# Two gated FFN blocks in one kernel: transposes of x and h moved from TensorE to VectorE blocks and DMAs

## The chip, the cores and the metric

One core of a Trainium2 chip runs the whole program. The metric is the device time of one execution in microseconds; the figure of a kernel is the median of its runs. TensorE is called PE, VectorE DVE, ScalarE ACT, GpSimd POOL, and SP (SyncE) issues the DMAs.

## The reference

x has 4 x 512 tokens of 512 values, 2048 rows in all. Two blocks follow each other, each of the form x + layernorm(FFN(layernorm(x))):

```python
def first(x):                                  # w_gate, w_up: 1376 x 512, w_down: 512 x 1376
    s = silu(x @ w_gate.T)
    s = set_to_zero(s, the 688 of each row's 1376 values with the smallest |s|)
    return (s * (x @ w_up.T)) @ w_down.T
def second(x):
    return (silu(x @ W_gate.T) * (x @ W_up.T)) @ W_down.T
x = x + layernorm(first(layernorm(x)))
x = x + layernorm(second(layernorm(x)))
```

All of it is float32. The selection by rank in the first block is exact.

## The kernel before, in words

**Precision.** A float32 matrix product is made of three fast ones: each operand is split into a high part (rounded by ACT) and a low part (the rest, subtracted by DVE), and hi x lo, lo x hi and hi x hi are added up in PSUM. So each operand costs an ACT instruction and a DVE instruction before PE can read it.

**First block.** The 2048 rows are 16 tiles of 128 tokens (`TILES`). For tile j: x is loaded into `xin` (two buffers), normalised (`x_stats`, L860; `x_normalise`, L871; POOL's `x_rstd`, L1193, in between), turned by four PE transposes into PSUM (`transpose_x`, L391), split into `xT` (`split_x_hi`, L632; `split_x_lo`, L877). `product(j, m, n)` (L404, matmuls at L418) makes gate (m=0) and up (m=1) in three column pieces n, 12 matmuls each, into a ring of four PSUM banks `gu_ps`. `silu` (L625) writes the gate into `prod` (two buffers), `abs_values` (L919) writes |s|, then a search for the 688th value runs: six passes `count` (L608) on ACT with two POOL instructions (`newton`, L1217) after each of five of them, then `find_below`, `find_top`, `find_flag` (L970, L976, L980) on DVE. `times_up` (L925) multiplies by up, and `select` (L1006, instruction at L1013) zeroes what is below the threshold, so that `prod` holds h. h is turned by eleven PE transposes into three PSUM banks `tr_ps` (`transpose_h`, L422, instruction at L432), split into the single buffer `hT` (`split_h_hi`, L647; `split_h_lo`, L888), and multiplied by w_down in 33 matmuls (`down`, L436, matmuls at L447) into the bank `y_ps`. Then come layernorm (`y_stats`, L895; `y_rstd`, L1200; `normalise_y`, L655), residual (`add_residual`, L904) and a store to a scratch tensor in HBM.

**Second block.** 16 tiles again, in four groups of four. Here the weights are the stationary operand, so h comes out turned already (`chunk`, L452, matmuls at L468; `down2`, L472, matmuls at L489). Only x has to be turned: four PE transposes per tile, into a bank of the ring. The weights of this block are loaded over those of the first (`load_pairs`, L272, from a copy that `copy_raw`, L264, made during the first block) and split on the way.

**Order of the work.** Nothing is scheduled by a program: each engine has its list of calls written out by hand, and semaphores tie them together. In the steady part of the first block (L524) PE's list for tile j is gate 0, gate 1, `transpose_h(j-2)`, gate 2, `down(j-2)`, `transpose_x(j+1)`, up 0, up 1, up 2. DVE's list is at L1084, ACT's at L740, POOL's at L1246 and SP's at L328. Tiles 11 to 14 (`TWO`) also prepare one x tile of the second block's first group each; the order in which x tiles are prepared is `XSEQ`.

Of the kernel before, what the change touches and what calls it, by code (L numbers as in the profile page):

```python
# [16 lines left out]
def sandwich(nc, x, w_gate, w_up, w_down, W_gate, W_up, W_down, out):  # L17
    B, S, H = x.shape
    I = w_down.shape[0]
# [29 lines left out]

    xf = x.rearrange("b s h -> (b s) h")  # L50
# [32 lines left out]

    def width(j):
        return P if j < JC - 1 else LASTJ

    ctx = ExitStack()
    with ctx:
# [26 lines left out]
        prod = sb("prod", [P, 2, IP])  # L115
# [46 lines left out]
        def h_place(idx):  # L162

            place = idx % 4
            if place < 2:
                return xT[:, place, 0, :], xT[:, place, 1, :]
            at = 2 * (place - 2) * GW
            flat = hT[:, :, :].rearrange("p s i -> p (s i)")
            return flat[:, at:at + GW], flat[:, at + GW:at + 2 * GW]
# [21 lines left out]
        g_done, u_done, x_tr, h_tr, y_done = map(sem, ("g_done", "u_done", "x_tr", "h_tr", "y_done"))  # L191
# [13 lines left out]
        half_done = sem("half_done")  # L205
        exact = sem("exact")
# [7 lines left out]

        ring = [("G", 0, 0), ("G", 0, 1), ("G", 0, 2), ("G", 1, 0), ("G", 1, 1), ("G", 1, 2)]
# [3 lines left out]
        X_AT = {2: 0, 4: 1, 6: 2, 8: 3}  # L219
        for g in range(GROUPS):  # L220
            for j in range(JC):
                ring += [("g", g * JC + j, 0), ("u", g * JC + j, 0)]
                if j in X_AT and g < GROUPS - 1:
                    ring.append(("X", TILES + GT * (g + 1) + X_AT[j], 0))
        place = {what: k for k, what in enumerate(ring)}

        def bank(what):
            return gu_ps[place[what] % 4]

        def x_bank(a):  # L230

            if ("X", a, 0) in place:
                return bank(("X", a, 0))
            return tr_ps[1] if a == 1 else tr_ps[2]

        @block.sync
        def _(sp):
# [3 lines left out]
            def load_x(a):  # L241

                p = POS[a]
                if p >= 2:
                    sp.wait_ge(x_tr, p - 1)
                if a >= TILES:
                    sp.wait_ge(stored[a % 2], 16 * ((a - TILES) // 2 + 1))
                src = rows(xf, a) if a < TILES else rows(x1, a - TILES)
                sp.dma_start(xin[:, p % 2, :], src).then_inc(x_in[p % 2], 16)

            def load_w(w):
# [7 lines left out]
                else:  # L259
                    size = P if n + c < JC else LASTJ  # L260
                    src = w_down[n * P:n * P + (c - 1) * P + size, :].rearrange("(c q) h -> q c h", q=size)
                    sp.dma_start(stage[0:size, slot, 0:c, :], src).then_inc(stage_in[slot], 16)
# [9 lines left out]
            def load_pairs(m):  # L272
# [4 lines left out]
                for k, (j, n) in enumerate(PAIRS):  # L277
# [46 lines left out]
            for w in range(12, NP):  # L324
                load_w(w)
            load_res(0)
            load_res(1)
            for j in range(2, TILES - 1):  # L328
                load_x(XSEQ[POS[j + 1] + 1])
                if j >= 4:  # L330
                    load_res(j - 2)
                if j in TWO:
                    load_x(XSEQ[POS[j + 1] + 2])
                store(j - 2)
                if j >= 3:
                    copy_raw(j - 3)
# [3 lines left out]
            load_pairs(1)  # L340
            store(TILES - 3)
            load_res(TILES - 2)
            store(TILES - 2)
# [3 lines left out]
            load_x(TILES + 6)  # L347
            load_x(TILES + 7)
            for g in range(GROUPS):
                b = TILES + GT * g  # L350
                if g > 0:
# [6 lines left out]
                    if g < GROUPS - 1:  # L358
                        load_x(b + 6)
                        load_x(b + 7)  # L360
                if g < GROUPS - 2:
                    load_x(b + 8)
                    load_x(b + 9)
# [10 lines left out]
        def _(pe):  # L374
            def bank_free(what):

                if place[what] < 4:
                    return
                kind, j, n = ring[place[what] - 4]
# [4 lines left out]
                elif kind == "X":  # L384
                    pe.wait_ge(xlo_done, POS[j] + 1)
# [4 lines left out]

            def transpose_x(a):  # L391
                p = POS[a]
                pe.wait_ge(xn_done, p + 1)
                if ("X", a, 0) in place:
                    bank_free(("X", a, 0))
                elif p >= 2:
                    pe.wait_ge(xlo_done, p)
                dst = x_bank(a)
                for c in range(KC):
                    last = nc.tensor.transpose(dst[:, c * P:(c + 1) * P],  # L400
                                               xin[:, p % 2, c * P:(c + 1) * P], ident[:, :])
# [20 lines left out]
            def transpose_h(j):  # L422

                x_before = TILES + GT if j >= TILES - 2 else POS[j + 2] + (2 if j + 1 in TWO else 1)
                pe.wait_ge(h_done, j + 1)
                for g, (c0, cn) in enumerate(TG):
                    if j >= 1:
                        pe.wait_ge(hlo_done, 3 * (j - 1) + g + 1)
                    if g == 2:
                        pe.wait_ge(xlo_done, x_before)  # L430
                    for c in range(cn):
                        last = nc.tensor.transpose(tr_ps[g][:, c * P:(c + 1) * P],  # L432
                                                   prod[:, j % 2, (c0 + c) * P:(c0 + c + 1) * P], ident[:, :])
                    last.then_inc(h_tr, 1)

            def down(j):  # L436
                if j >= 1:
                    pe.wait_ge(res_done, j)
                if j == 0:
                    pe.wait_ge(wlo_done, NP)  # L440
                for g, (c0, cn) in enumerate(TG):
                    pe.wait_ge(hlo_done, 3 * j + g + 1)
                    for c in range(c0, c0 + cn):
                        k = width(c)
                        hhi, hlo = (hT[0:k, s, c * P:(c + 1) * P] for s in range(2))
                        for i, (h, w) in enumerate(((hhi, down_lo), (hlo, down_hi), (hhi, down_hi))):
                            last = nc.tensor.matmul(y_ps[:, :], h, w[0:k, c, :],  # L447
# [24 lines left out]
            def down2(g, j, tiles, last_tile=True):  # L472
# [6 lines left out]
                for r in tiles:  # L479
# [5 lines left out]
                    elif j == 0:  # L485
                        pe.wait_ge(hlo_done, 3 * (TILES - 1) + r + 1)
# [31 lines left out]
            transpose_h(0)  # L518
            product(2, 1, 0)
            product(2, 1, 1)  # L520
            down(0)
            transpose_x(3)
            product(2, 1, 2)
            for j in range(3, TILES - 1):  # L524
                product(j, 0, 0)
                product(j, 0, 1)
                transpose_h(j - 2)
                product(j, 0, 2)
                down(j - 2)
                transpose_x(j + 1)  # L530
                product(j, 1, 0)
                product(j, 1, 1)
                if j in TWO:
                    transpose_x(XSEQ[POS[j + 1] + 1])
                product(j, 1, 2)
            product(TILES - 1, 0, 0)
            product(TILES - 1, 0, 1)
            transpose_h(TILES - 3)
            product(TILES - 1, 0, 2)
            for n in range(3):  # L540
                product(TILES - 1, 1, n)
            down(TILES - 3)
            transpose_h(TILES - 2)
            chunk(0, 0, 0)
            chunk(0, 0, 1)
            down(TILES - 2)
            chunk(0, 1, 0)
            chunk(0, 1, 1)
            transpose_h(TILES - 1)
            chunk(0, 2, 0)  # L550
            down(TILES - 1)
            chunk(0, 2, 1)
            transpose_x(TILES + GT)
            chunk(0, 3, 0)
            chunk(0, 3, 1)
# [759 lines left out]
```

## Time and profile before

| what | value |
|---|---|
| median of 3 runs | 786.13 us (786.05 to 786.14) |
| the profiled execution, its own time | 787.0 us |
| its span, first to last instruction | 785.0 us |
| PE busy | 766.9 us, 98% of the span |
| DVE, ACT, POOL busy | 406.5, 346.5, 117.8 us |
| mean granted TensorE clock | 0.997 |
| DMA | 51.18 MB, 22,338 packets |

The span is the part of the execution that the trace covers; some 2 us of the execution lie outside of it. Busy time of an engine is the union of its instructions. A share of busy time is an average over stages: first block to about 371 us, a passage with the new weights to about 440 us, second block after that.

### The profile page before, as it was taken

Reading aid. Unit: us, or ns where it says so; the run is one execution under the profiler, and the core shown is the slowest. Engines: PE = TensorE matmul, PEld = TensorE weight load, DVE = VectorE, ACT = ScalarE, POOL = GpSimd, SP = SyncE. Lnnn points to the kernel's source line nnn. Section 1 sums busy time; section 2 is a strip of 40 time slices with the busy share of each in tenths; the row PEclk is TensorE's granted clock in tenths of the full one; section 3 lists DMA queues with packets and bytes.
Section 4 is the critical chain, followed back from the end, with each engine's and each line's share of the span. In section 5 each row is a group of like instructions: output and inputs, shape, how many; then the busy total and the mean of one; then the engine's idle time right before and its main releaser. Section 6 shows DMA issues by size and latency. Waiting matters only on the chain.

```text
span 785.0 us, 9833 instructions
## 1 busy us (share of the span) xinstructions
PE 766.9 (98%) x3593; PEld 646.2 (82%) x3593; DVE 406.5 (52%) x822; ACT 346.5 (44%) x575; POOL 117.8 (15%) x278
## 2 busy tenths in 40 slices
PE   8999999999999999999989999999999999999996
PEld 7888888888888888889877788788878888788884
DVE  7686766766667666785783443253224332151114
ACT  6787665656656666566843221131112111131112
POOL 0533321122211222212310000010001000010001
PEclk9999999999999999999999999999999999999999
DMA  8520102222022220223713101020010210021001
GB/s 288 165 74 28 45 32 77 77 77 76 2 77 77 76 91 28 77 78 103 276 43 137 59 15 40 1 94 15 13 41 28 67 41 1 0 93 42 0 1 54
DMA packets 22338, 51.18 MB, mean 65 GB/s; under 512 B 2320, under 2 KB 5904, under 8 KB 22096
## 3 DMA queue, kind: packets, MB, share of 16 engines
q1 hardware_dynamic: 22288, 50.54, 19.3%
q8 instruction: 28, 0.46, 0.3%
q14 instruction: 22, 0.18, 0.1%
HBM read 42.14 MB, written 16.84 MB: 75 GB/s over the span
## 4 chain that ended last, share of the span: by engine, by line
PE 83%; DVE 7%; ACT 3%; issue 3%; POOL 2%; DMA 1%; DVEq 0%; POOLq 0%; SPq 0%; ACTq 0%
PE gu_ps L468 29%; PE gu_ps L418 23%; PE y_ps L447 13%; PE tr_ps L489 11%; PE y_ps L489 4%; PE tr_ps L432 2%; ACT junk L617 1%; PE tr_ps L400 1%; DMA xin<-in_L_attn_x 1%; PE gu_ps L400 1%; DVE below L973 1%; POOL thr L1224 1%; POOL move L1221 1%; DVE gate_lo L846 1%; DVE up_lo L858 0%
## 5 line engine op out<-in xcount | busy, mean ns | idle before, releaser
L617 ACT ACTIVATE junk<-absv,thr 128x1383 bf16<-128x1383 f32 x96 | 139.3, 1451 | 57.9 <-POOL thr L1224 56.4
L1023 DVE TENSOR_TENSOR prod<-gu_ps,prod 128x512 f32<-128x512 f32 (+1 forms) x44 | 30.4, 690 | 182.9 <-PE gu_ps L468 182.9
L418 PE MATMUL gu_ps<-up_hi,xT 128*128 128x460 f32 (+1 forms) x384 | 111.3, 371 | 0.0
L418 PE MATMUL gu_ps<-gate_hi,xT 128*128 128x460 f32 (+1 forms) x384 | 111.1, 370 | 0.0
L447 PE MATMUL y_ps<-down_hi,hT 128*128 128x512 f32 (+1 forms) x352 | 110.3, 395 | 0.0
L673 ACT ACTIVATE prod<-gu_ps 128x512 f32<-128x512 f32 (+1 forms) x44 | 26.3, 597 | 127.4 <-PE gu_ps L468 127.4
L447 PEld LDWEIGHTS y_ps<-down_hi,hT 128*128 128x128 f32 (+1 forms) x352 | 66.9, 190 | 15.0
L418 PEld LDWEIGHTS gu_ps<-gate_hi,xT 128*128 128x128 f32 x384 | 72.2, 188 | 7.8
L418 PEld LDWEIGHTS gu_ps<-up_hi,xT 128*128 128x128 f32 x384 | 72.2, 188 | 7.7
L447 PE MATMUL y_ps<-down_lo,hT 128*128 128x512 f32 (+1 forms) x176 | 70.3, 399 | 4.5 <-DVE hT L892 4.4
L418 PE MATMUL gu_ps<-up_lo,xT 128*128 128x460 f32 (+1 forms) x192 | 73.2, 381 | 1.5 <-DVE up_lo L846 0.8
L418 PE MATMUL gu_ps<-gate_lo,xT 128*128 128x460 f32 (+1 forms) x192 | 73.0, 380 | 1.6 <-DVE xT L886 1.2
L1205 POOL TENSOR_TENSOR yrstd<-yvar,half 128x1 f32<-128x1 f32 x32 | 18.7, 585 | 247.4 <-DVE yvar L902 246.5
L468 PE MATMUL gu_ps<-xg_even,gate_hi 128*128 128x512 f32 (+1 forms) x176 | 54.5, 391 | 0.0
L468 PE MATMUL gu_ps<-xg_odd,gate_hi 128*128 128x512 f32 (+1 forms) x176 | 54.5, 391 | 0.0
L468 PE MATMUL gu_ps<-xg_even,up_hi 128*128 128x512 f32 (+1 forms) x176 | 54.3, 390 | 0.0
L468 PE MATMUL gu_ps<-xg_odd,up_hi 128*128 128x512 f32 (+1 forms) x176 | 54.2, 389 | 0.0
L1198 POOL TENSOR_TENSOR xrstd<-xvar,half 128x1 f32<-128x1 f32 x32 | 18.6, 583 | 206.1 <-DVE xvar L869 206.0
L683 ACT ACTIVATE xT<-prod 128x512 fp32r<-128x512 f32 (+1 forms) x22 | 13.9, 633 | 67.5 <-DVE prod L1023 67.5
L447 PEld LDWEIGHTS y_ps<-down_lo,hT 128*128 128x128 f32 (+1 forms) x176 | 33.5, 190 | 12.3 <-issue 2.9
L1221 POOL TENSOR_SCALAR move<-sgn 128x1 f32<-128x1 f32 x80 | 29.1, 364 | 87.2 <-ACT junk L617 87.2
L418 PEld LDWEIGHTS gu_ps<-gate_lo,xT 128*128 128x128 f32 x192 | 36.1, 188 | 6.5 <-issue 1.6
(115 smaller groups left out, 1370.3 us busy)
## 6 DMA issues: line engine op xcount, KB each, us to landing
xin<-x_scratch SPq DMA_DIRECT2D x18, 256.0 KB, 3.2
xin<-in_L_attn_x SPq DMA_DIRECT2D x16, 256.0 KB, 4.6
xres<-in_L_attn_x SPq DMA_DIRECT2D x16, 256.0 KB, 4.8
x_scratch<-xres SPq DMA_DIRECT2D x16, 256.0 KB, 2.0
xres<-x_scratch SPq DMA_DIRECT2D x14, 256.0 KB, 2.8
out<-xres SPq DMA_DIRECT2D x14, 256.0 KB, 2.1
raw<-in_L_ffn_W_gate SPq DMA_DIRECT2D x4, 688.0 KB, 4.9
raw<-in_L_ffn_W_up SPq DMA_DIRECT2D x4, 688.0 KB, 4.7
```

The costliest lines, as they stand in the source:

```text
L400: last = nc.tensor.transpose(dst[:, c * P:(c + 1) * P], xin[:, p % 2, c * P:(c + 1) * P], ident[:, :])
L418: last = nc.tensor.matmul(dst[:, 0:CW[n]], xt, w, start=(c == 0 and i == 0), stop=(c == KC - 1 and i == 2))
L432: last = nc.tensor.transpose(tr_ps[g][:, c * P:(c + 1) * P], prod[:, j % 2, (c0 + c) * P:(c0 + c + 1) * P], ident[:, :])
L447: last = nc.tensor.matmul(y_ps[:, :], h, w[0:k, c, :], start=(c == 0 and i == 0), stop=(c == JC - 1 and i == 2))
L468: last = nc.tensor.matmul(dst[0:k, :], w, xt[:, s, c, :], start=(c == 0 and i == 0), stop=(c == KC - 1 and i == 2))
L489: last = nc.tensor.matmul(y_bank(b)[:, :], h[0:k, toks], w[0:k, j, :], start=(j == 0 and i == 0), stop=(j == JC - 1 and i == 2))
L617: nc.scalar.activation(junk[:, 0:I + PAD], absv[:, q, 0:I + PAD], ACT.Sign, bias=thr[:, q:q + 1], scale=-1.0, accum_out=sgn[:, q:q + 1]).t ...
L673: nc.scalar.activation(prod[0:k, 0, 0:GW], bank(("g", idx, 0))[0:k, :], ACT.Silu).then_inc(s2_done, 1)
L1023: nc.vector.tensor_tensor(prod[0:k, 0, GW:2 * GW], bank(("u", idx, 0))[0:k, :], prod[0:k, 0, 0:GW], ALU.mult).then_inc(p2_done, 1)
L1198: nc.gpsimd.tensor_tensor(xrstd[:, :], xvar[:, :], half[:, :], ALU.pow).then_inc(xr_done, 1)
L1205: nc.gpsimd.tensor_tensor(yrstd[:, q:q + 1], yvar[:, q:q + 1], half[:, :], ALU.pow).then_inc(yr_done, 1)
L1221: stepped(nc.gpsimd.tensor_scalar(move[:, :], sgn[:, q:q + 1], sgn[:, q:q + 1], float((WINDOW - 1) ** 2) + 0.5, ALU.mult, ALU.is_gt))
```

## The change

Of the x tiles the first five in `XSEQ` (`FIRST`) stay with PE; the other 27, and all 16 h tiles, are turned without it. DVE transposes the 32 x 32 blocks of the buffer in place (`xin`, or `prod` with its 1408 columns), and four DMAs from SBUF to SBUF, one for each band of 32 partitions, put the blocks in place: each takes 32 partitions with 16 (x) or 44 (h) runs of 32 values (128 bytes) and writes 128 partitions with 4 or 11 runs of 128 bytes. What arrives is a transposed tile whose contraction rows stand in another order, so the rows of w_gate, w_up, W_gate, W_up and w_down are laid out in that order on the host, and the first five x tiles get a copy with reordered columns (`x_first`). The DMAs land in the low half of `xT`, of the group buffer or of `hT`, from which ACT makes the high part and DVE the low part in place. The last chunk of `down` has 128 rows in place of 96, padded with zeros. The three `tr_ps` banks join the ring of product banks in the first block (5, then 6, then 7 of them). `down(j-2)` moves behind up 0; lists of all engines are reordered. Parts of the second block's h that stood in `hT` go to `h_two`, which shares memory with `prod`.

```diff
+            def move_x(a):
+                sp.wait_ge(xswap_done, moved(a) + 1)
+                if a < TILES:
+                    sp.wait_ge(u_done, U_AT[a - 2, 2])
...
+                for q in range(4):
+                    src = xin[q * BLK:(q + 1) * BLK, POS[a] % 2, :].rearrange("p (b t) -> p b t", t=BLK)
+                    sp.dma_start(raw_x[:, :, q * BLK:(q + 1) * BLK].bitcast(F32), src).then_inc(
+                        x_moved[POS[a] % 2], 16)
+            def move_h(j):
+                sp.wait_ge(hswap_done, j + 1)
+                if j >= 1:
+                    sp.wait_ge(y_done, j)
+                raw_h = hT[:, 1, :].rearrange("p (c t) -> p c t", c=JC)
+                for q in range(4):
+                    src = prod[q * BLK:(q + 1) * BLK, j % 2, :].rearrange("p (b t) -> p b t", t=BLK)
+                    sp.dma_start(raw_h[:, :, q * BLK:(q + 1) * BLK].bitcast(F32), src).then_inc(h_moved, 16)
...
     SP, tiles 3 to 14 (before: load_x, load_res, [load_x], store, copy_raw)
                 if j >= 4:
                     load_res(j - 2)
+                a = XSEQ[POS[j + 1]:]
                 if j in TWO:
+                    load_x(a[2])
+                move_h(j - 1)
+                if j > 3:
+                    move_x(a[1])
+                if 3 < j and j not in TWO:
+                    load_x(a[2])
+                elif j in TWO and a[2] < TILES + GT:
+                    load_x(a[3])
+                    move_x(a[2])
                 store(j - 2)
+                copy_raw(j - 3)
...
     PE, tiles 4 to 15 (before: see L524)
+            for j in range(4, TILES):
+                for n in range(3):
+                    product(j, 0, n)
+                for n in range(3):
+                    product(j, 1, n)
+                    if n == max(6 - j, 0) and j < TILES - 1:
+                        down(j - 2)
...
     ACT
             def silu(j, n):
                 act.wait_ge(g_done, G_AT[j, n])
                 if j >= 2:
-                    act.wait_ge(h_tr, 3 * (j - 2) + n + 1)
+                    act.wait_ge(h_moved, 64 * (j - 1))
...
             def split_h_hi(j):
+                act.wait_ge(h_moved, 64 * (j + 1))
+                for c0, cn in TG:
+                    cols = slice(c0 * P, (c0 + cn) * P)
+                    nc.scalar.activation(hT[:, 0, cols], hT[:, 1, cols].bitcast(F32), ACT.Copy).then_inc(hhi_done, 1)
...
     DVE
+                if p >= FIRST:
+                    dve.wait_ge(xn_done, p + 1)
+                    nc.vector.transpose(xin[:, p % 2, :], xin[:, p % 2, :]).then_inc(xswap_done, 1)
+            def swap_h(j):
+                dve.wait_ge(h_done, j + 1)
+                nc.vector.transpose(prod[:, j % 2, :], prod[:, j % 2, :]).then_inc(hswap_done, 1)
...
     DVE, tiles 3 to 14, as the list stands after the change
                 find_below(j - 1)
                 find_top(j - 1)
                 if j > 3:
                     split_h_lo(j - 2)
                 abs_values(j)
                 if j - 1 in TWO:
                     split_x_lo(TILES + j - 1 - TWO[0])
                 if j > 3:
                     x_stats(a[1])
                 find_flag(j - 1)
                 select(j - 1)
                 if j > 3:
                     x_normalise(a[1])
                 swap_h(j - 1)
                 if j > 4:
                     split_x_lo(j + 1)
                 if j in TWO:
                     x_stats(a[2])
                 y_stats(j - 2)
                 times_up(j, 0)
                 if j in TWO:
                     x_normalise(a[2])
                 add_residual(j - 2)
                 times_up(j, 1)
                 times_up(j, 2)
```

Here `a = XSEQ[POS[j + 1]:]`, so a[1] is x tile j+2 up to tile 10. At the start `down(0)` stands behind gate 0 of tile 3 (before: behind up 1 of tile 2); at the end `down(14)` stands behind two pairs of chunks and `down(15)` behind two more.

## Rows read from the trace of the kernel before

**Rows 1.** The page, parts 1 and 2: busy us; granted PE clock.

```profile
PE 766.9 (98%) x3593; PEld 646.2 (82%) x3593; DVE 406.5 (52%) x822; ACT 346.5 (44%) x575; POOL 117.8 (15%) x278
...
PEclk9999999999999999999999999999999999999999
```

**Rows 2.** Windows: one steady tile, one of tiles 11 to 14; busy us.

```profile
206.70:231.00 24.30, 24.30 (x121) 21.27 (x121) 15.73 (x34) 15.05 (x26) 4.97 (x15) 1.00 0.18 62
304.30:329.00 24.70, 24.70 (x126) 21.65 (x125) 17.48 (x38) 15.54 (x27) 5.52 (x16) 1.00 0.21 72
```

**Rows 3.** Chain of waits, steady part: start us, us, what.

```profile
206.24 0.44 PE tr_ps L400 x4
206.68 12.58 PE gu_ps L418 x60
219.26 1.20 PE tr_ps L432 x11
220.47 2.49 PE gu_ps L418 x12
222.95 7.59 PE y_ps L447 x33
```

**Rows 4.** Chain of waits, a tile of 11 to 14; second block.

```profile
309.34 0.44 PE tr_ps L400 x4
...
446.52 0.44 PE gu_ps L400 x4
```

**Rows 5.** Groups by shape: the PE transposes and the last chunk of down.

```profile
L432 PE MATMUL tr_ps<-ident,prod 128*128 128x128 f32 x176 | 21.8, 272 | 0.0
...
L400 PE MATMUL tr_ps<-ident,xin 128*128 128x128 f32 x80 | 12.1, 273 | 1.3 <-DVE xin L874 1.3
...
L400 PE MATMUL gu_ps<-ident,xin 128*128 128x128 f32 x48 | 7.2, 272 | 0.0
...
L447 PE MATMUL y_ps<-down_hi,hT 96*128 96x512 f32 x32 | 10.1, 397 | 0.0
```

**Rows 6.** Waits of PE: us in total, times, longest us.

```profile
PE y_ps L447 <- DVE hT L892: 4.4, 2, 2.3
```

**Rows 7.** DVE in order, one steady tile: start us, us, instruction.

```profile
216.59 1.65 DVE L973 SCALAR_TENSOR_TENSOR below<-absv,thr 128x1376 f32<-128x1376 f32 x1 [0.51 <-POOL thr L1224]
...
220.87 1.75 DVE L892 TENSOR_TENSOR hT<-tr_ps,hT 128x512 fp32r<-128x512 f32 x3 [1.00 <-ACT hT L652]
223.57 1.59 DVE L922 SCALAR_TENSOR_TENSOR absv<-prod 128x1376 f32<-128x1376 f32 x1 [0.95 <-ACT prod L629]
...
228.18 1.65 DVE L1013 SCALAR_TENSOR_TENSOR prod<-absv,kth,prod 128x1376 f32<-128x1376 f32 x1 [0.87 <-DVE anyflag L1004]
229.75 0.69 DVE L865 BATCH_NORM_STATS2 xstat<-xin 128x6 f32<-128x512 f32 x1
```

**Rows 8.** ACT in order, the same tile.

```profile
220.25 1.47 ACT L652 ACTIVATE hT<-tr_ps 128x512 fp32r<-128x512 f32 x3
...
222.99 0.55 ACT L629 ACTIVATE prod<-gu_ps 128x456 f32<-128x456 f32 x1 [0.83 <-PE gu_ps L418]
```

**Rows 9.** One line: DVE's 32-column block transpose, ns min/median/max.

```profile
L997 DVE STREAM_TRANSPOSE flagT<-flag x16: 211/212/214, 44.3 to 399.1; 128x32 f32<-128x32 f32 x16
```

**Rows 10.** Groups by shape: a DVE instruction on one column.

```profile
L983 DVE TENSOR_SCALAR rank<-sgn 128x1 f32<-128x1 f32 x16 | 2.3, 146 | 0.0
```

**Rows 11.** DMA, 424 to 435 us, 2048-byte packets; then 371 to 388.5 us.

```profile
DMA packets 1760, 3.34 MB, mean 304 GB/s; under 512 B 128, under 2 KB 128, under 8 KB 1760
...
q1 hardware_dynamic: 1760, 3.34, 87.8%
...
DMA packets 1731, 5.67 MB, mean 324 GB/s; under 512 B 192, under 2 KB 448, under 8 KB 1728
...
q1 hardware_dynamic: 1728, 5.64, 90.1%
```

**Rows 12.** The page, part 6: issues, KB each, median us to landing.

```profile
x_scratch<-xres SPq DMA_DIRECT2D x16, 256.0 KB, 2.0
```

More of the change, by code:

```diff
@@ L82, in sandwich, with moved @@
     HALF = H // 2
+    BLK = 32
+    def moved(a):
+        return POS[a] - FIRST
     def width(j):
@@ L114, in sandwich @@
         xres = sb("xres", [P, 2, H])
-        prod = sb("prod", [P, 2, IP])
+        with nc.sbuf_tensor("prod", [P, 2, IP], F32) as prod:
+            pass
+        h_two = sb("h_two", [P, 2, IP], F32R)
         junk = sb("junk", [P, IA], BF16)
@@ L339, in _ @@
             load_pairs(0)
-            load_pairs(1)
+            load_pairs(1, range(2))
+            move_h(TILES - 2)
+            load_pairs(1, range(2, NPAIR))
             store(TILES - 3)
             load_res(TILES - 2)
+            move_x(TILES + 4)
+            move_h(TILES - 1)
+            load_x(TILES + 6)
             store(TILES - 2)
@@ L374, in _, with taken_out @@
         def _(pe):
[L375 to L379, printed above, removed]
+            def taken_out(what):
+                kind, j, n = what
                 if kind == "G":
@@ L389, in bank_free @@
                     pe.wait_ge(p2_done, j + 1)
+            def bank_free(what):
+                if before[what] is not None:
+                    taken_out(before[what])
             def transpose_x(a):
[L392 to L397, printed above, removed]
+                pe.wait_ge(xn_done, a + 1)
+                if a >= 2:
+                    pe.wait_ge(xlo_done, a - 1)
                 dst = x_bank(a)
@@ L517, in _ @@
                 product(2, 0, n)
-            transpose_h(0)
-            product(2, 1, 0)
-            product(2, 1, 1)
+            transpose_x(3)
+            for n in range(3):
+                product(2, 1, n)
+            product(3, 0, 0)
             down(0)
[L522 to L535, printed above, removed]
@@ L542, in _ @@
             down(TILES - 3)
-            transpose_h(TILES - 2)
-            chunk(0, 0, 0)
-            chunk(0, 0, 1)
+            for j in range(2):
+                chunk(0, j, 0)
+                chunk(0, j, 1)
             down(TILES - 2)
[L547 to L550, printed above, removed]
+            for j in range(2, 4):
+                chunk(0, j, 0)
+                chunk(0, j, 1)
             down(TILES - 1)
-            chunk(0, 2, 1)
@@ L779, in _ @@
             normalise_y(last - 2)
+            split_h_hi(last - 1)
             split_pair_hi(NPAIR + 1)
@@ L1114, in _ @@
             select(last - 1)
+            swap_h(last - 1)
             split_pair_lo(0)
```

439 lines of the change are left out of this document (236 added, 203 removed).

## The prediction

> **What bounds the kernel now.** The page comes first: PE is busy for 766.9 of 785.0 us at a granted clock of nine tenths or more in all slices, DVE for 52% [rows 1]. The windows of single tiles show the same: PE fills all of a 24.30 us tile of the first block, and all of a 24.70 us tile among 11 to 14, while DVE has 15.73 and 17.48 us of work and ACT about 15 [rows 2]. Then the chain of waits, which says what that PE time is. In the steady part it never leaves PE: 0.44 us for four transposes of x, 12.58 us for five products, 1.20 us for the eleven transposes of h, 2.49 us for the sixth product, 7.59 us for down [rows 3]. A tile of 11 to 14 has a second 0.44, and so has every x tile turned in the second block [rows 4]. PE waits for others very little: the largest is 4.4 us in two waits for h in the passage between the blocks [rows 6]. So PE is the bound, and what leaves its list shortens the time as long as nothing else becomes the bound.
>
> **What is removed.** All 16 h tiles leave PE: 16 x 1.20 = 19.2 us [rows 3]. Of 32 x tiles 27 leave: 27 x 0.44 = 11.9 us [rows 3, 4]. The chain's figures are taken, not the 272 ns by which the groups list one of the 176 + 128 transposes [rows 5], since these overlap. Sum: **31.1 us**. A steady tile then asks PE for 24.30 - 1.20 - 0.44 = 22.66 us, one of tiles 11 to 14 for 24.70 - 1.20 - 0.88 = 22.62 us. The last chunk of down gets 128 rows in place of 96. That costs nothing: it took 397 ns with 96 rows [rows 5], and the full ones differ by a few ns.
>
> **DVE gets the block transposes.** The trace has one form of it, 32 columns in 212 ns [rows 9], against 146 ns for an instruction on one column [rows 10]. If all of the difference goes by columns, it is 2.1 ns a column, and 1408 columns take 3.1 us and 512 take 1.2. If it is the filling of the block, a column costs what it costs elsewhere, 1.65 us for 1376 [rows 7], so 1.7 us for h and 0.6 for x. I take these, since a long instruction is nearest to them. DVE then has 15.73 + 1.7 + 0.6 = 18.0 us of work in a steady tile, and 17.48 + 1.7 + 1.2 = 20.4 in a tile of 11 to 14, against 22.6. Hidden by PE, but in four tiles with little cover; at the dear price these would need 17.48 + 3.1 + 2.4 = 23.0 us plus DVE's own waits, some 1 to 1.5 us over PE's each.
>
> **The DMAs are the unknown.** An h tile is 5632 runs of 128 bytes, 352 for each of 16 DMA engines; an x tile 128 for each. No packet of data in the trace is that small. Two stretches of dense traffic give a line. From 424 to 435 us, 87.8% of 16 x 11 us went into 1760 - 128 = 1632 packets of 2048 bytes, 94.7 ns each. From 371 to 388.5 us, 90.1% of 16 x 17.5 us went into 1728 - 192 = 1536 packets of 5.64 MB / 1536 = 3672 bytes, 164 ns each [rows 11]. So 0.0427 ns a byte and 7.3 ns a packet: 128 bytes would take **12.8 ns**. The bounds are 7.3 ns (no cost of bytes) and 94.7 ns (no cheaper than 2048 bytes). I take the line. What lies around the data: a 256 KB store takes 2.0 us to land [rows 12], 8 x 94.7 ns = 0.8 of it data, so 1.2 us, and 0.4 for SP's wait and issues; the last three issues run beside the first one's data. From `swap_h` to landed h: D = 1.6 + 352c, with c = 12.8 ns 6.1 us.
>
> **Where a slow move would show.** `silu(j,0)` waits for h of tile j-2 to be moved out of `prod`, and behind it on ACT stand `split_h_hi` and two more silus. Behind them stand `abs_values`, the flag, `select` and `swap_h` of the next h. That is a loop, once round per tile. From landing: silus and high part 0.55 + 1.47 + 0.55 + 0.55 = 3.1 us [rows 8]; `abs_values` 1.6; `x_stats` 1.1 (0.69 and two small ones); flag and its load 228.18 - 223.57 - 1.59 = 3.0; `select` 1.65 [rows 7]; `x_normalise` 0.6 by its 512 columns; the two swaps 2.3. Sum 13.3 us, and D closes it. With D = 6.1 it is 19.4 us, under PE's 22.66: hidden, with 3.3 us to spare. It equals 22.66 at c = 22 ns and the old 24.30 at c = 26.7 ns.
> The second condition is `hT`, a single buffer: `move_h(j-1)` waits for `down(j-2)` to end, and `down(j-1)` starts one period less 7.59 us later, 15.1 us. D and a first high and low part of some 1.3 us must fit in. At 6.1 us they do. The search loop (`abs_values` to `find_below`, 240.89 - 223.57 = 17.3 us with the period added, then top, low parts and the next `abs_values`, 24.30 less the idle 0.51, 1.00 and 0.95 = 21.8) fits in 22.66 as well [rows 7], and the x statistics no longer hold up POOL in the middle of it.
> SP's list: behind `move_h` stand `move_x`, loads and a store. `move_x` waits for up 2 of the tile and has half a tile until the split; the store has a tile until `load_res` wants its buffer. x moves add 128 packets, 1.6 us. All hidden.
>
> **Start and passage.** At the start `down(0)` waits for a DMA more, but two products more stand ahead of it. In the passage the 4.4 us of waits for h [rows 6] meet 5.5 us or so more PE work ahead of each `down`, against 7.8 us more of swap and move and a queue of weight loads. The additional product banks take away waits under 1 us. I count half of the 4.4 as regained and as much lost at the start and in tiles 11 to 14: zero, plus or minus 4.
>
> **The sum.** The profiled execution took 787.0 us for a span of 785.0; the median is 786.1, 0.9 under it. 787.0 - 31.1 = 755.9; as a median **755.0 us**.
>
> **The rivals.**
> 1. *Small packets are dear, slower than before.* h lands late, ACT and DVE wait, and the loop sets the period from c = 26.7 ns on. For it: no row has such a packet, 32 source partitions feed 128, and the line is drawn from packets 16 times as long. Against it: 7.3 ns is all that the rows leave for a packet's fixed part. At c = 29 ns D is 11.8 and the loop 25.1 us, 0.8 over the old period in eight tiles, 1.1 or so in the four with two x tiles: 786 + 11 - 12 x 0.44 of the second block, which stays won = 792. At c = 58 ns it is 35.3 us: some 910. The Trainium skill, page DMA: Bandwidth & Descriptors, section Specifications, says that below 512 bytes the engines read, modify and write and miss their rate; were 128 bytes to cost what 512 do, that is this rival with its 29 ns. The same page, section Why small descriptors are slow (HBM only), exempts SBUF to SBUF and would leave the forecast as it is; no run here shows either yet. Chance 0.26.
> 2. *Between the two*, c from 22 to 26.7 ns: a part is given back, up to 1.64 us in each of 12 tiles: 757 to 779. Chance 0.15, with 0.03 more for a result within 0.2% of before, about what a measurement can tell from no change.
> 3. *DVE becomes the bound in tiles 11 to 14*, at the dear price of the swap or since its waits add up to more than 2 us: 4 x 1.5 us, and the loop is 1.9 us longer elsewhere but still under PE: 761. Chance 0.10.
> 4. *The waits are regained too*, and the clock stays up in the passage: 750 to 752. This is the low end; chance 0.06, in the forecast's 0.46.
>
> **The numbers.** Forecast 0.46 (750 to 758), DVE 0.10, between 0.15: faster 0.71. Same 0.03, slower 0.26. The range from 750 to 800 leaves out a little below and the slow cases from c = 31 ns on, some 0.18 together.
>
> **What the profile will show.** Right: no line for h transposes on PE, 20 transposes of x; the chain in the steady part on PE alone, with a period of 22.66 us; PE at 98% again; block transposes of 1408 columns at 1.7 us; h moves landing within 6 to 7 us of the issue. Wrong: a period above 22.7 us with silu waiting for the DMA into `hT`, or PE's down for `hT`. A DMA share of the slices of five tenths or more in the first block would mean packets of 25 ns or more. A DVE without idle time in tiles 11 to 14 would be rival 3.

## The result, and the profile after

The changed kernel takes 765.52 us (median of 4 runs, 763.45 to 766.78) against 786.09 us for the kernel before, measured beside it: a ratio of 0.9732 [0.9714, 0.9749]. It is 20.6 us faster, where 31.1 were forecast. The direction and the range were right; a third of the gain is missing. The profiled execution took 766.78 us, with a span of 765.0 us.

The page of the kernel after, parts 1 and 2, to be read beside [rows 1]:

```profile
PE 740.0 (97%) x3309; PEld 622.0 (81%) x3309; DVE 449.5 (59%) x865; ACT 347.5 (45%) x575; POOL 127.6 (17%) x278
...
PE   8998999899999999999997999999999999999996
...
PEclk9999999999999999999998999999999999999999
DMA  8532445445455545576951422031121211130001
...
DMA packets 170530, 69.85 MB, mean 91 GB/s; under 512 B 150480, under 2 KB 154064, under 8 KB 170288
```

PE is busy for 26.9 us less, and stands idle for 765.0 - 740.0 = 25.0 us in place of 18.1. So the spans' difference of 20.0 us is 26.9 less 6.9 of new idle time. The 26.9 in turn is the 31.1 of the forecast less time at a lower clock. Ahead of PE's last stretch of work the granted clock of the kernel after is at half rate (1.2 in place of 2.4 GHz) in three intervals, 3.41 us from 61.8, 3.41 from 143.7 and 6.83 from 406.5 us; the kernel before has one of 3.41 us, from 414.4. The windows around the first two, with the columns of [rows 2]:

```profile
60.40:70.00 9.60, 9.58 (x36) 7.86 (x37) 8.41 (x24) 6.70 (x13) 1.71 (x5) 0.82 0.13 47
143.00:157.00 14.00, 13.78 (x58) 12.17 (x59) 11.73 (x25) 10.06 (x19) 2.96 (x9) 0.88 0.78 162
```

An interval costs half of its length where PE works in it. Of the 6.83 us, 1.6 lie in a wait and cost nothing, so the kernel after loses 1.7 + 1.7 + 2.6 = 6.0 us and the kernel before 1.7. 31.1 - 4.3 - 6.9 = 19.9, and the spans differ by 20.0.

The steady part is what the forecast said. The chain of waits after, start us, us, what (beside [rows 3]):

```profile
177.64 7.55 PE y_ps L517 x33
185.20 5.00 PE gu_ps L502 x24
190.19 2.52 PE tr_ps L502 x12
192.71 5.02 PE gu_ps L502 x24
197.73 2.52 PE tr_ps L502 x12
200.25 7.55 PE y_ps L517 x33
```

The chain never leaves PE, and there are no transposes in it. The period is 200.25 - 177.64 = 22.61 us, forecast 22.66. Windows after (length, busy us of PE, PEld, DVE, ACT and POOL, granted clock, DMA share, GB/s): most of the first block, one steady tile, one of tiles 11 to 14, beside [rows 2].

```profile
143.20:363.50 220.30, 220.28 (x1018) 192.52 (x1019) 180.39 (x359) 149.60 (x259) 63.49 (x139) 0.99 0.57 122
177.60:200.20 22.60, 22.60 (x107) 19.70 (x106) 18.31 (x38) 15.37 (x27) 6.22 (x15) 1.00 0.53 118
320.00:342.60 22.60, 22.60 (x107) 19.71 (x106) 20.16 (x42) 15.58 (x27) 7.24 (x15) 1.00 0.59 121
```

From 143 to 363 us PE is without a gap, in tiles 11 to 14 too. So what is missing was lost ahead of and behind this stretch. PE's waits after (us in total, times, longest), beside [rows 6]:

```profile
PE y_ps L517 <- DVE hT L949: 7.7, 3, 5.6
PE tr_ps L502 <- ACT prod L685: 2.5, 1, 2.5
PE gu_ps L502 <- DVE xT L943: 1.9, 1, 1.9
PE gu_ps L538 <- DVE up_lo L910: 1.8, 1, 1.8
```

The 5.6 us are the wait of down(15) in the passage. At the start there are 2.5 us at 57.9, two waits for h at 108.6 and 129.6 us (2.0 together) and 1.9 for x at 141.3. Starts of down before and after show the sizes: down(4) starts at 150.05 us before and 155.04 after. Ahead of it the transposes of five h tiles (6.0 us) and of two x tiles (0.9) are gone, and one product (2.5) has come, so 145.7 was due: it is 9.4 us late. 4.5 of these are idle time of PE, 3.4 the lower clock, and the other 1.5 are additional busy time of PE for which the sum has no term. From down(12) to the first matmul of the second block's `down2` it is 89.5 us before and 93.3 after, where 0.8 more was due for the chunks moved there: **3 us lost in the passage, 9.4 at the start**, the lower clock among both. From down(4) to down(12) it is 0.4 us less than was due, and the rest of the second block is 13.9 us shorter where 13.0 was due: 9.4 + 3.0 - 0.4 - 0.9 = 11.1 us, the difference between 31.1 and 20.0.

The largest wait of the start, at 57.9 us, is not a matter of the DMAs alone. `silu(2,0)` stands behind the search of tile 1 in ACT's list, and that search waits 3.67 us for two POOL instructions which take 2.02 and 2.22 us where their medians are 0.29 and 0.34:

```profile
51.20 4.61 DVE L898 TENSOR_TENSOR down_lo<-stage,down_hi 128x1024 fp32r<-128x1024 f32 x4
51.59 2.02 POOL L1296 TENSOR_SCALAR move<-sgn 128x1 f32<-128x1 f32 x1 [1.92 <-ACT junk L673]
53.72 2.22 POOL L1299 TENSOR_SCALAR thr<-move,step,thr 128x1 f32<-128x1 f32 x1
```

They run beside four subtractions of the weight split on DVE, in the kernel before too (1.50 and 1.69 us at 50.8). That these subtractions make them slow was not tested.

### The profile page after: what moved, and what is told of

Same layout as the page of the kernel before. It is cut to its first block, busy times and chain, and to the rows that moved or that the text cites. A ratio compares the mean times of both kernels' runs of the same rounds, so it can differ in the third digit from the quotient of the medians.

```text
span 765.0 us, 9433 instructions
## 1 busy us (share of the span) xinstructions
PE 740.0 (97%) x3309; PEld 622.0 (81%) x3309; DVE 449.5 (59%) x865; ACT 347.5 (45%) x575; POOL 127.6 (17%) x278
## 4 chain that ended last, share of the span: by engine, by line
PE 75%; DVE 8%; issue 5%; ACT 4%; DMA 3%; POOL 2%; SPq 2%; DVEq 0%; POOLq 0%; ACTq 0%
PE gu_ps L538 29%; PE tr_ps L559 12%; PE gu_ps L502 11%; PE y_ps L517 11%; PE tr_ps L502 9%; PE y_ps L559 4%; SPq L310 2%; DMA hT<-prod 2%; ACT junk L673 1%; POOL thr L1299 1%; DVE prod L1070 1%; DVE hT L949 1%; POOL move L1296 1%; DMA xin<-in_L_attn_x 1%; DVE prod L934 1%
## 5 line engine op out<-in xcount | busy, mean ns | idle before, releaser
L517 PE MATMUL y_ps<-down_hi,hT 128*128 128x512 f32 x352 | 111.0, 397 | 0.0
L517 PEld LDWEIGHTS y_ps<-down_hi,hT 128*128 128x128 f32 x352 | 67.5, 192 | 14.9
L517 PE MATMUL y_ps<-down_lo,hT 128*128 128x512 f32 x176 | 70.7, 402 | 7.7 <-DVE hT L949 7.7
L502 PE MATMUL gu_ps<-up_hi,xT 128*128 128x460 f32 (+1 forms) x240 | 69.5, 371 | 0.0
L502 PE MATMUL gu_ps<-gate_hi,xT 128*128 128x460 f32 (+1 forms) x232 | 68.8, 378 | 0.0
L502 PEld LDWEIGHTS gu_ps<-gate_hi,xT 128*128 128x128 f32 x232 | 45.0, 194 | 5.1
L517 PEld LDWEIGHTS y_ps<-down_lo,hT 128*128 128x128 f32 x176 | 33.9, 193 | 16.1 <-issue 8.8
L502 PE MATMUL gu_ps<-gate_lo,xT 128*128 128x460 f32 (+1 forms) x116 | 44.5, 384 | 1.9 <-DVE xT L943 1.9
L738 ACT ACTIVATE xT<-prod 128x512 fp32r<-128x512 f32 (+1 forms) x22 | 13.9, 632 | 69.8 <-DVE prod L1080 62.7
L502 PE MATMUL gu_ps<-up_lo,xT 128*128 128x460 f32 (+1 forms) x120 | 44.8, 373 | 0.4 <-DVE prod L986 0.4
L502 PE MATMUL tr_ps<-gate_hi,xT 128*128 128x460 f32 (+1 forms) x152 | 44.9, 377 | 0.0
```

Of the source, the lines that this page charges most:

```text
L502: last = nc.tensor.matmul(dst[:, 0:CW[n]], xt, w, start=(c == 0 and i == 0), stop=(c == KC - 1 and i == 2))
L517: last = nc.tensor.matmul(y_ps[:, :], h, w[:, c, :], start=(c == 0 and i == 0), stop=(c == JC - 1 and i == 2))
L738: nc.scalar.activation(h_place(idx)[0][0:k, :], prod[0:k, 0, GW:2 * GW], ACT.Copy).then_inc(h2hi_done, 1)
```

## The moves, measured

The block transposes on DVE, in the groups by shape after (count, busy us, mean ns, idle before):

```profile
L934 DVE STREAM_TRANSPOSE prod<-prod 128x1408 f32<-128x1408 f32 x16 | 25.9, 1616 | 0.1
L930 DVE STREAM_TRANSPOSE xin<-xin 128x512 f32<-128x512 f32 x27 | 19.2, 712 | 0.9
L1054 DVE STREAM_TRANSPOSE flagT<-flag 128x32 f32<-128x32 f32 x16 | 3.4, 212 | 0.5
```

1.62 and 0.71 us: the cheap price of the prediction (1.7 and 0.6). The dear one, 2.1 ns a column, would have shown 3.1 us.

The DMAs are another matter. SP, DVE and ACT around one move of h after (start us, us, instruction):

```profile
96.39 1.65 DVE L934 STREAM_TRANSPOSE prod<-prod 128x1408 f32<-128x1408 f32 x1
...
98.06 5.30 SPq L310 DMA_DIRECT2D hT<-prod  x4
...
107.22 0.56 ACT L685 ACTIVATE prod<-tr_ps 128x460 f32<-128x460 f32 x1 [1.44 <-DMA hT<-prod]
```

The swap ends at 98.04, SP needs 5.30 us only to issue the four DMAs, and `silu`, which waits for them and for nothing else in its last 1.44 us, starts at 107.22. So **D is 9.2 us here**, where 6.1 was forecast; from the end of a swap to the landing of the last band it is 8.3 to 9.6 us in tiles 0 to 13, 11.4 in tile 14 and 9.6 in tile 15. In the dense part of this move, 99.3 to 106.3 us, the view of the DMA shows:

```profile
DMA packets 5730, 0.86 MB, mean 123 GB/s; under 512 B 5660, under 2 KB 5660, under 8 KB 5730
...
q1 hardware_dynamic: 5730, 0.86, 80.2%
```

The 16 engines are marked busy for 0.802 x 16 x 7 = 90 us, 15.7 ns a packet; but the packets take 16 x 7 / 5730 = **19.5 ns each as they follow each other**. The forecast's 12.8 ns was near the busy time and left out the gaps between packets. With 19.5 ns the 352 packets of an engine take 6.9 us in place of 4.5, and what lies around them takes 2.3 in place of 1.6.

The loop of the prediction then reads 13.3 + 9.2 = 22.5 us. The ends of the swaps of tiles 2 to 5 bear it out: 98.04, 120.50, 141.99 and 163.73, periods of 22.46, 21.49 and 21.74 us against PE's 22.6. It is still hidden, so the steady part shows nothing of it. But the spare 3.3 us have shrunk to about one or less, and spare time is what makes up for a late start.

## The experiments

Differences in us are between medians, each against the 765.52 of the kernel after. That kernel was not timed again with them, but the kernel before was, at 785.92 us (experiments 1, 2, 3 and 6) and 786.21 us (the others) against 786.09, and the ratios are to it. The mean granted clock of every run is known too, and (1 - clock) x span is what a run lost by the lower clock, with an interval at its end that stands behind PE's last work: on average 6.7 us in the four runs of the kernel after, 3.1 in those of the kernel before.

**1. The loop made 1.2 us shorter.** DVE turns h before it normalises and turns the next x tile (`x_normalise` holds both, 0.54 and 0.71 us).

```diff
+                swap_h(j - 1)
                 if j > 3:
                     x_normalise(a[1])
-                swap_h(j - 1)
```

The same for `swap_h(1)` and `x_normalise(4)` at the start.

> Edit: on VectorE, swap_h(j-1) stands ahead of x_normalise(a[1]) and its block transpose, so that h can be moved about 1.25 us earlier in every tile of the first block. Theory A (the round from a landed h over silu, abs_values, select and swap_h to the next landed h, 13.3 + 8.5 to 9.1 us, sets the pace of tiles 2 to 6, where TensorE waits 8 us in all, and is just hidden by TensorE's 22.6 us later): the round gets 1.25 us shorter, the waits of the start shrink and the median falls by 2 to 6 us, to 760 to 763.5. Theory B (the start is lost to the load of weights and to the clock, not to the move of h): within 1 us of 765.5. The steady period stays 22.6 us under both.

Measured: 762.14 us (760.62 to 762.35), ratio 0.9684 [0.9668, 0.9699]: 3.4 us faster. The swaps of tiles 2 to 5 now end 21.18, 20.35 and 21.35 us apart. Where the last wait of the start ends, PE is 0.8 us ahead of the kernel after (142.4 against 143.2 us). Down(6) starts 2.4 us earlier (197.89, after: 200.25), since the interval of half rate that stands behind that wait in the kernel after, worth 1.7 us, is absent here. Experiments 6 and 7 have the start of the kernel after unchanged, 8 has this one. So there are three profiled executions with the old start, whose last wait ends at 142.8 to 144.1 us, all with that interval behind it, and two with the new one, 141.4 and 142.4 us, both without. That the shorter loop brings the start forward is thus shown; how much of it is idle time and how much clock is not. Over all runs the lower clock costs 5.5 us here against 6.7, a third of the gain. The wait in the passage stays at 5.6 us.

**2. A larger move.** A fifth DMA with 1408 runs, to a scratch tensor in HBM, in each `move_h`; `silu` waits for it too.

```diff
+                extra = prod[0:BLK, j % 2, :].rearrange("p (b t) -> p b t", t=BLK)
+                sp.dma_start(beside.rearrange("(p b) t -> p b t", p=BLK)[:, :, 0:BLK], extra).then_inc(beside_in, 16)
```

> Edit: ahead of the four DMAs of each move_h a fifth of the same size (1408 runs of 128 bytes, from prod to a scratch tensor in HBM, with its own semaphore, for which silu waits too). Theory A (the move of h, 8.5 to 9.1 us, is within 1 us of being the bound in the steady part): the round grows by a quarter of the data time, 1.3 to 1.8 us, to 23.2 to 23.7 us, over TensorE's 22.6; 12 tiles at 0.6 to 1.1 us and some at the start: 8 to 15 us more, 773 to 780. Theory B (DMAs are hidden by several us in the steady part): 0 to 2 us more.

Measured: 776.25 us (three runs, 775.45 to 776.68; a fourth of 1894.91 us is left out), ratio 0.9868 [0.9846, 0.989]: 10.7 us slower. PE's waits in it:

```profile
PE y_ps L523 <- DVE hT L957: 10.9, 8, 4.1
PE tr_ps L508 <- ACT prod L692: 2.9, 1, 2.9
PE gu_ps L544 <- DVE up_lo L918: 2.0, 1, 2.0
```

Three waits for h have become eight, and they reach through the steady part: the first matmul of down starts 0.8 us after the one ahead of it at 157.3 us, 1.1 at 203.9 and 0.8 at 318.5. The move's four bands land 9.2 to 10.6 us after the swap in tiles 2 to 13, and five of the eight periods from down(4) to down(12) are 0.4 to 1.0 us longer than 22.6. So with a quarter more packets the loop holds PE up in most tiles: the spare time is about as small as the loop's sum says. But these periods are 3.5 us of the 10.7; the rest is lost at the start and in the passage, and the lower clock costs 9.8 us here against 6.7.

**3. The same bytes in 11 times longer runs.** The move of h copies 1408-byte runs. The blocks of h land in wrong places, so this part of the result isn't the reference's.

```diff
-                    src = prod[q * BLK:(q + 1) * BLK, j % 2, :].rearrange("p (b t) -> p b t", t=BLK)
-                    sp.dma_start(raw_h[:, :, q * BLK:(q + 1) * BLK].bitcast(F32), src).then_inc(h_moved, 16)
+                    src = prod[q * BLK:(q + 1) * BLK, j % 2, :].rearrange("p (b t) -> p b t", t=part)
+                    sp.dma_start(hT[:, 1, q * part:(q + 1) * part].bitcast(F32), src).then_inc(h_moved, 16)
```

> Edit: move_h copies the same bytes in runs of 1408 bytes (128 runs per DMA in place of 1408), so that what lands in hT is h with its blocks in other places. Theory A (the price is in the number of runs: descriptors and packets, 7 us of data for 5632 of them): the move takes 4 to 5 us in place of 8.5 to 9.1, the start loses its waits and the median falls by 6 to 10 us, to 755.5 to 759.5. Theory B (the fixed part of four DMAs or the bytes set the price): the move gets less than 1.5 us shorter and the median stays within 2 us. Theory C (the move is fast enough, the start is lost elsewhere): the move gets shorter and the median stays within 1.5 us.

Measured: 757.34 us (757.14 to 758.83), ratio 0.9636 [0.9621, 0.9651]: 8.2 us faster. Part 6 of the page and the packets:

```profile
DMA packets 88610, 69.85 MB, mean 92 GB/s; under 512 B 60368, under 2 KB 72144, under 8 KB 88368
...
hT<-prod SPq DMA_DIRECT2D x64, 176.0 KB, 3.3
```

A DMA lands 3.3 us after its issue (after: 4.8), an issue takes SP 0.61 us in the median, and `silu` no longer waits for a DMA. From the swap to landed h it is 5.3 to 7.0 us in tiles 0 to 13, for 8.3 to 9.6. Both waits for h at the start are gone, and the one in the passage is 4.1 us. So the number of packets, not the bytes, sets the price of the move. Down(4) starts 5.3 us earlier than in the kernel after: of the 9.4 us lost at the start 5.3 hang on the move of h, and 4 are lost with a fast move too. Among these is the wait of 2.5 us at 57.9, which stays, since ACT's list comes to `silu(2,0)` at that time anyway. No version here removed it.

**4. Two queues.** Two of the four bands of h in tiles 2 to 13 are issued from ACT's queue.

```diff
-                for q in range(4):
+                for q in range(2 if 3 <= j + 1 < TILES - 1 else 4):
...
+                    act.dma_start(raw_h[:, :, q * BLK:(q + 1) * BLK].bitcast(F32), src).then_inc(h_moved, 16)
```

> Edit: for h of tiles 2 to 13 two of the four bands are issued from ScalarE's DMA queue, ahead of count(j,3), the other two from SP as now. Theory A (the data time of the move, 7 us for 5632 packets, is the 16 DMA engines' at 14 ns a packet and their gaps, and the issuing queue adds gaps in the first 1.5 us only): the move gets 1 to 2 us shorter, ScalarE's search 1.3 us longer, the median falls by 0 to 3 us. Theory B (one queue's issue, with stalls of 2 to 3 us, sets the move): it gets 3 us or more shorter and the start gains 4 us or more.

Measured: 780.83 us (779.33 to 781.54), ratio 0.9925 [0.9911, 0.9938]: 15.3 us slower, which neither theory had. PE's waits, and part 6 of the page:

```profile
PE y_ps L517 <- DVE hT L958: 14.0, 10, 3.7
PE gu_ps L502 <- DVE prod L995: 4.0, 1, 4.0
...
hT<-prod SPq DMA_DIRECT2D x40, 176.0 KB, 4.9
hT<-prod ACTq DMA_DIRECT2D x24, 176.0 KB, 6.5
```

One issue takes ACT 0.62 to 3.4 us, the two of a tile 1.6 to 4.2 together, amid the search that the loop waits for, and the DMAs land no sooner: the last band 8.7 to 10.0 us after the swap in tiles 2 to 13. Two issuers don't feed the engines faster here. That the 5.3 us of SP's issues are mostly a wait for room among the packets fits this and experiment 3, but was not measured by itself.

**5. Five banks in place of seven** in the first block: the two later `tr_ps` banks don't join the ring.

```diff
-            if what == ("G", 2, 0):
-                line = [tr_ps[2]] + line
-            elif what == ("G", FIRST, 0):
-                line = [tr_ps[1]] + line
-            elif what == ("g", 0, 0):
+            if what == ("g", 0, 0):
```

> Edit: the part 'seven product banks' undone down to five: tr_ps[1] and tr_ps[2] never join the ring of product banks of the first block. Theory A (more banks let TensorE run on while ScalarE's silu and VectorE's times_up wait for the move of h): without them TensorE waits for silu or times_up in every tile from 3 on where the move is late; up to 1 us a tile, 768 to 780. Theory B (banks are free in time anyway, as before with four): within 1 us of 765.5.

Measured: 766.29 us (765.55 to 768.2), ratio 0.9746 [0.9731, 0.976]; 0.8 us over after, less than the two spreads. PE waits 5.0 us for `silu` at 55.8 us, in place of the 2.5 at 57.9, and 1.9 more at 86; the later waits of the start for h and most of that for x vanish. PE waits earlier or later for the same loop; more banks move the wait. They may do more than that: the granted clock is lower here in all five runs (0.986 to 0.988, after: 0.989 to 0.993), 10.4 us lost against 6.7, so a difference in idle time can hide behind the clock.

**6. The order in the passage.** SP moves h of tile 15 ahead of x tile 20, and ACT and DVE do the layernorm of tile 14 and the split of h of tile 15 ahead of the third chunk's silu and product; the layernorm goes ahead of the splits of two pairs of weights as well. The lines of SP and of ACT's `split_h_hi`:

```diff
-            move_x(TILES + 4)
             move_h(TILES - 1)
+            move_x(TILES + 4)
...
+            split_h_hi(last)
             silu2(2)
             split_h2_hi(2)
-            split_h_hi(last)
```

> Edit: in the passage between the blocks move_h(15) stands ahead of move_x(20) on SP; ScalarE and VectorE normalise y of tile 14 and split h of tile 15 ahead of the third chunk's h of the second block. Nothing else moves. Theory A (the 5.6 us wait of down(15) comes from the lists of ScalarE and VectorE, and the wait brings half clock for 6.8 us behind it): the wait falls under 1 us, half clock goes too, 5 to 8 us less, 757.5 to 760.5. Theory B (the landing of h15 behind down(14) in the single buffer hT is what is late): the wait stays at 3 us or more and the median falls by less than 3 us.

The wait as it stands in the kernel after, on SP, DVE and PE (start us, us, instruction):

```profile
391.06 2.65 SPq L300 DMA_DIRECT2D xg_odd<-xin  x4
393.80 4.95 SPq L310 DMA_DIRECT2D hT<-prod  x4
...
404.64 0.69 DVE L974 TENSOR_TENSOR xres<-y_ps,xres 128x512 f32<-128x512 f32 x1 [1.90 <-ACT y_ps L710]
405.25 0.68 DVE L1080 TENSOR_TENSOR prod<-gu_ps,prod 128x512 f32<-128x512 f32 x1
406.63 0.69 DVE L1087 TENSOR_TENSOR h_two<-prod,h_two 128x512 fp32r<-128x512 f32 x1 [0.70 <-ACT h_two L738]
407.24 1.29 DVE L949 TENSOR_TENSOR hT<-hT 128x512 fp32r<-128x512 f32 x2
...
408.07 0.77 PE L517 MATMUL y_ps<-down_lo,hT 128*128 128x512 f32 x1 [5.61 <-DVE hT L949]
```

The x move holds SP for 2.65 us in front of the h move, and in front of `split_h_lo` (L949) stand the residual and a chunk's product and split. Measured with the new order: 758.29 us (756.72 to 758.71), ratio 0.9639 [0.9623, 0.9655], 7.2 us faster. The wait is 0.9 us, and the start is unchanged. Of the spans' 8.5 us 4.7 are this wait and 1.3 the one for `up_lo` ahead of it (1.8, now 0.5); the rest fits the interval of half rate behind it, 6.83 us long and gone here, which the next experiment takes by itself. Over all runs the lower clock costs 2.8 us less than in the kernel after. Which of the three lists brings how much was not taken apart.

**7. The wait filled.** The order as after, but PE does 48 transposes of the identity into a free bank ahead of down(15).

```diff
             down(TILES - 1)
...
+            taken_out(in_y_bank[0])
+            for _ in range(48):
+                nc.tensor.transpose(tr_ps[0][:, 0:P], ident[:, :], ident[:, :])
```

> Edit: 48 transposes of the identity into a free PSUM bank ahead of down(15), in the 5.6 us in which TensorE waits for h15. They add no work of the kernel. Theory A (half clock for 6.8 us follows that wait because TensorE stood still): the wait is filled, the clock stays whole, and the median falls by 1.5 to 3 us. Theory B (half clock there has another cause): the same 6.8 us at half clock, and the median stays or rises by up to 0.5 us.

Windows of after (the 8.07 us up to down(15), and down(15)), where the columns are as above:

```profile
400.00:408.07 8.07, 2.47 (x11) 1.72 (x11) 5.41 (x10) 3.37 (x7) 0.83 (x2) 0.90 0.47 120
408.07:418.33 10.26, 10.26 (x34) 8.22 (x35) 5.33 (x8) 3.70 (x6) 0.00 (x0) 0.74 0.00 1
177.64:185.19 7.55, 7.55 (x35) 6.20 (x34) 6.32 (x22) 4.79 (x8) 3.39 (x6) 1.00 0.22 76
```

and of the kernel with the filled wait, in the same place:

```profile
402.50:412.00 9.50, 9.15 (x65) 8.25 (x64) 6.87 (x12) 7.08 (x12) 0.83 (x2) 1.00 0.24 78
```

After the wait down takes 10.26 us at a granted clock of 0.74, part of it at 1.2 GHz, where it takes 7.55 at 2.4 GHz. With the wait filled the clock stays at 1.00. The time is 763.09 us (760.37 to 764.39), ratio 0.9695 [0.9676, 0.9714], 2.4 us less than after though PE does 5.4 us of useless work. So the lower clock came of the idle time. The interval made down 2.7 us longer (10.26 against 7.55); the shift of 2.4 is of that size, though the two spreads overlap by 0.9 us, and over all runs the lower clock costs 4.3 us here against 6.7, again 2.4. The other profiled executions agree: where down(15) waited 2.1 to 5.6 us for h (before, after and experiments 1 to 5) an interval of half rate lies at the end of the wait or behind it, and where it waited 0.4 to 0.9 (experiments 6, 7 and 8) there is none.

**8. Both reorderings**, experiments 1 and 6 together.

> Edit: h_swap_first and passage together. Each took away waits of its own stage (3.4 and 7.2 us by the medians), so if the stages are independent the sum is 765.5 - 3.4 - 7.2 = 754.9 us, between 753.5 and 756.5. If the passage's gain hung on where the first block ends relative to the weight loads, it is less: 757 or more.

Measured: 755.54 us (754.87 to 756.30), ratio 0.9608 [0.9594, 0.9621]: 10.0 us faster than after and 30.7 faster than before. The two gains add up (10.0 of 10.6). Against experiment 6 the shorter loop lets the last wait of the start end 1.3 us earlier (141.4, there 142.8), and again no half-rate interval stands behind it (1.7). Down(4) starts at 151.7 us, still 6 later than the 145.7 that were due. From down(12) to `down2` it takes 85.3 us, 5.0 less than the 89.5 + 0.8 that were due: PE is idle for 1.8 us in it where the kernel before was for 5.0, and that kernel's interval of half rate, 1.7, is gone too. So the new order of the passage does more than undo what the change had cost there. Its page, its waits, and its windows of the long stretch and of down(15):

```profile
PE 736.0 (98%) x3309; PEld 618.8 (82%) x3309; DVE 449.5 (60%) x865; ACT 347.2 (46%) x575; POOL 128.2 (17%) x278
```

```profile
PE tr_ps L502 <- ACT prod L685: 2.6, 1, 2.6
PE gu_ps L502 <- DVE xT L943: 1.8, 1, 1.8
PE y_ps L569 <- DVE prod L884: 1.7, 1, 1.7
PE y_ps L517 <- DVE hT L949: 1.6, 3, 0.9
```

```profile
143.20:363.50 220.30, 220.30 (x1026) 192.27 (x1025) 182.23 (x364) 152.28 (x262) 63.81 (x141) 1.00 0.60 132
400.00:408.00 8.00, 8.00 (x37) 6.55 (x36) 6.16 (x10) 4.99 (x8) 0.00 (x0) 1.00 0.35 100
```

## Why the prediction was right in direction and 10.5 us short

**The bound and what was removed: right.** PE was the bound, and the chain's durations, not the groups' 272 ns, were the ones to take. The period came out at 22.61 us against 22.66, in tiles 11 to 14 at 22.60 against 22.62, and the second block became 13.9 us shorter, where 13.0 was due.

**DVE: right.** 1.62 and 0.71 us; 18.31 and 20.16 us of work in the two kinds of tile against 18.0 and 20.4 forecast. Rival 3 (761 us) did not come about, since PE had no gap in tiles 11 to 14.

**The DMA: the price of a packet was the first term mis-sized.** The prediction took 12.8 ns from a line through busy times; the records show at most 15.7 ns busy and 19.5 ns from packet to packet. That is D = 9.2 us in place of 6.1, 8.3 to 9.6 over tiles 0 to 13; "within 6 to 7 us of the issue" did not come about. The busy share of a queue says how long packets lie on the engines, not how fast they follow each other. Rivals 1 and 2 set in at 26.7 and 22 ns, and rival 2 missed narrowly: experiment 2, which adds a quarter to the packets, is close to it. Of the two sections of the Trainium skill's page DMA: Bandwidth & Descriptors, the one named Why small descriptors are slow (HBM only), which exempts SBUF to SBUF, is the nearer one: were 128 bytes to cost what 512 do, the line would have given 29 ns, and the trace has 15.7 busy. But the exemption doesn't mean that runs are free: the dense part of the move has 123 GB/s where the 2048-byte packets of [rows 11] have 304, and longer runs gain 8.2 us in experiment 3.

**The loop: the sum was right and the conclusion too kind.** The 13.3 us of its other members measured 13.3 (107.22 to 120.50). With 9.2 it closes at 22.5 where 3.3 us of spare time were forecast. This costs nothing in the steady part. It costs at the start, where the loop has to catch up: experiment 3 puts 5.3 us on it.

**"Start and passage: zero, plus or minus 4": the step that failed.** It was about 12 us against the change, 9.4 at the start and 3 in the passage, of which 1.3 came back elsewhere. By kind the 11.1 us that are left are 6.9 of PE's idle time and 4.3 of lower clock. At the start the prediction set two more products ahead of `down(0)` against "a DMA more"; that did not cover the moves that follow, each of them dearer than forecast. The prediction had both ingredients of the passage in view ("7.8 us more of swap and move", the queues) and weighed them against 5.5 us of additional PE work, without following SP's, ACT's and DVE's lists through the place, where the x move and a chunk's instructions stood ahead of h. Nor did it price the clock outside of rival 4, though the kernel before had 3.41 us at half rate in the same passage. Experiment 8 puts a number on it: two reorderings, which remove no work, gain 10.0 us. That this lands at 755.54 us, beside the forecast's 755.0, is partly luck: the passage is then 5 us better than was due, and the start is still 6 us worse.

**The range.** 765.5 us lies between 750 and 800, but above the 750 to 758 that the forecast itself was given. It lies in the 757 to 779 of rival 2, and did not come about as rival 2 has it, by a longer steady period. The range held because it was made wide for slow packets, and not because of what was said of the start and the passage.

**One sign was worked out wrongly.** "A DMA share of five tenths or more in the first block would mean packets of 25 ns or more": the share is 0.53 in a steady tile with 0.18 before. (0.53 x 22.6 - 0.18 x 24.3) x 16 = 122 us over 5632 + 2048 packets is 15.8 ns. By the same working 25 ns would have shown 0.72.

**The banks.** "Waits under 1 us" was right; experiment 5 could not tell their absence from noise, with a lower clock in its way.

**What stays open.** How the 9.4 us of the start divide between idle time and clock is only known for single executions: the half-rate intervals fall in other places from one execution to the next, and runs of one kernel differ by up to 4.0 us. The profiled execution of the kernel after has the lowest clock of its four runs, so the 4.3 us are rather high for it: with the intervals at the end counted too it lost 5.9 us more than the kernel before, and over all runs that is 3.6 on average. The wait at 57.9 us, 2.5 us or more, is in every version, and an order that keeps POOL's two instructions apart from the weight split wasn't tried.

## What to carry to other kernels

When work is moved off the bound engine, write down the loop that the moved work closes, and ask not only whether it fits under the period but how much is left: a loop with less than a microsecond to spare can't make up for a late start or for a passage, and every place where the steady order begins or ends has to be followed list by list. Price a strided DMA by its runs and by the time from packet to packet, and put its issue, which here took as long as the half of the move, first in its queue. Look at the granted clock behind each wait of PE: here 5.6 us of waiting for h were followed by a down that took 2.7 us longer.

## What the runs showed that was not expected

- 128-byte packets between SBUF and SBUF: 15.7 ns busy, 19.5 ns from one to the next on each engine, 5632 of them in 8.3 to 9.6 us from the end of the swap to the last landing (tiles 0 to 13).
- The issue of one DMA with 1408 runs takes SP 0.61 to 3.2 us (5.3 us for four); in 1408-byte runs its median is 0.61 us. With two of the four issued from ACT, these two cost ACT up to 4.2 us together and landed in 6.5 us, those of SP in 4.9.
- Intervals of half clock of 3.41 and 6.83 us stood at or behind waits of PE, though not behind each: the 2.5 us at 57.9 us had one in the kernel after (granted clock 0.82 from 60.4 to 70 us) and none in experiments 1 and 7. With the 5.6 us in the passage filled by transposes, the clock stayed whole there.
- Two POOL instructions of one column took 2.02 and 2.22 us, beside four subtractions of 128x1024 on DVE, in place of 0.29 and 0.34.
